# Six up products of the first shared unit moved beside the last attention batch

## The reference

```python
q = (layernorm(x) @ Wq.T) * scale ; k = ctx @ Wk.T ; v = ctx @ Wv.T      # 16 heads of 16
scores = sigmoid(einsum('blhd,bshd->bhls', q, k))                       # 8 x 16 x 512 x 1601
x = x + einsum('bhls,bshd->blhd', scores, v).reshape(B, L, E) @ Wo.T
n = layernorm(x)
# 16 experts: each takes its 64 best tokens of every batch (softmax of n @ gate_w.T)
h = gelu(x_tok @ Wg.T) * (x_tok @ Wu.T) ; out[tokens] += (h @ Wd.T) * weight
# one shared expert over all tokens
shared = (gelu(n @ Ws_g.T) * (n @ Ws_u.T)) @ Ws_d.T
return x + out + shared
```

## Time and profile before

| | |
|---|---|
| median of three runs | 1318.85 us (1317.76 to 1321.44) |
| profiled execution | 1318.16 us, span 1316.2 us |
| mean granted TensorE clock | 0.996 |
| PE busy | 1288.5 us (98%), 10172 matmuls |
| ACT busy | 984.2 us (75%) |
| DVE busy | 725.8 us (55%) |
| POOL busy | 285.6 us (22%) |
| chain that ended last | PE 85%, ACT 6%, DVE 3%, issue 3%, DMA 2% |

### The profile page before, as it was taken

One profiled execution on the slowest core, in us unless ns is written; L12 is line 12 of the kernel. 1 busy time (PEld: TensorE's weight loads), 2 busy tenths in 40 slices (PEclk: granted clock), 3 DMA queues, 4 the chain that ended last, 5 costly groups with the idle time before them and its releaser, 6 DMA issues.

```text
span 1316.2 us, 25441 instructions
## 1 busy us (share of the span) xinstructions
PE 1288.5 (98%) x10172; PEld 772.7 (59%) x10172; DVE 725.8 (55%) x1371; ACT 984.2 (75%) x1148; POOL 285.6 (22%) x288
## 2 busy tenths in 40 slices
PE   8899999999999999999999999999999999999997
PEld 6455444354444544444444453226888888888887
DVE  6375375376357437537535633204559777777773
ACT  4678999989998998998999889995232355555553
POOL 2000020021003002002000200220000567777635
PEclk9899999999999999999999999999999999999999
DMA  7784885775777587478567648624533577777854
GB/s 227 153 181 141 134 172 169 118 156 166 138 134 192 128 129 172 156 126 153 169 129 154 138 103 129 134 82 144 193 123 103 179 200 190 190 188 190 195 109 48
DMA packets 119637, 198.67 MB, mean 151 GB/s; under 512 B 22592, under 2 KB 71744, under 8 KB 119520
## 3 DMA queue, kind: packets, MB, share of 16 engines
q1 hardware_dynamic: 99680, 163.08, 52.5%
q0 software_dynamic: 19648, 33.72, 12.5%
q10 hardware_dynamic: 192, 0.26, 0.1%
HBM read 120.22 MB, written 63.47 MB: 140 GB/s over the span
## 4 chain that ended last, share of the span: by engine, by line
PE 85%; ACT 6%; DVE 3%; issue 3%; DMA 2%; SPq 1%; POOL 0%; POOLq 0%; DVEq 0%; ACTq 0%
PE score L1786 19%; PE score L1699 17%; PE acc L1728 13%; PE misc L1728 13%; PE score L1804 10%; ACT probs L860 6%; PE score L1530 5%; PE score L1544 5%; PE score L1553 1%; DMA keys<-key_scr 1%; PE score L1571 1%; SPq L548 1%; PE score L1634 0%; DMA norm_t_scr<-nt_lo 0%; POOL out L798 0%
## 5 line engine op out<-in xcount | busy, mean ns | idle before, releaser
L860 ACT ACTIVATE probs<-score 128x1024 f32<-128x1024 f32 (+1 forms) x832 | 788.4, 1034 | 84.6 <-PE score L1699 78.8
L1699 PE MATMUL score<-queries,keys 48*128 48x512 f32 (+1 forms) x1664 | 313.1, 439 | 13.4 <-DMA keys<-key_scr 5.6
L1699 PEld LDWEIGHTS score<-queries,keys 48*128 48x128 f32 (+1 forms) x1664 | 139.0, 180 | 288.0 <-ACT probs L860 220.6
L1728 PE MATMUL acc<-probs,values 128*32 128x512 f32 (+1 forms) x1664 | 212.4, 603 | 0.5 <-ACT probs L860 0.2
L1728 PE MATMUL misc<-probs,values 128*32 128x512 f32 (+1 forms) x1664 | 207.1, 600 | 2.0 <-ACT probs L860 0.9
L1004 DVE TENSOR_REDUCE whole<-score 128x512 f32<-128x1024 f32 (+1 forms) x75 | 77.0, 1026 | 205.3 <-PE score L1530 128.6
L713 POOL DMA_DIRECT2D ctx_raw<-ctx_t x32 | 23.4, 733 | 653.0 <-DVE ctx_lo L982 569.3
L870 ACT ACTIVATE gelu<-score 128x512 f32<-128x512 f32 (+1 forms) x100 | 57.2, 582 | 96.0 <-PE score L1786 95.4
L785 POOL DMA_INDIRECT gathered<-norm_scr,gather_row x64 | 81.3, 1270 | 197.2 <-DVE gather_row L1337 181.4
L1786 PE MATMUL score<-tok_hi,gu_hi 128*128 128x512 f32 (+1 forms) x400 | 120.7, 383 | 0.0
L1786 PE MATMUL score<-tok_lo,gu_hi 128*128 128x512 f32 (+1 forms) x400 | 120.0, 381 | 0.0
(11 more groups left out here) (248 smaller groups left out, 1563.6 us busy)
## 6 DMA issues: line engine op xcount, KB each, us to landing
keys<-key_scr SPq DMA_DIRECT2D x186, 200.2 KB, 7.9
key_scr<-key_parts SPq DMA_DIRECT2D x45, 512.0 KB, 8.1
gu_raw<-w_gu SPq DMA_DIRECT2D x17, 1024.0 KB, 6.8
ctx_raw<-ctx_t POOLq DMA_DIRECT2D x24, 512.0 KB, 5.1
queries<-query_scr SPq DMA_DIRECT2D x180, 64.0 KB, 2.8
d_raw<-w_d SPq DMA_DIRECT2D x17, 512.0 KB, 8.7
query_scr<-query_parts SPq DMA_DIRECT2D x15, 512.0 KB, 9.0
norm<-xn SPq DMA_DIRECT2D x224, 32.0 KB
```

The costliest lines, as they stand in the source:

```text
L860: act.activation(probs[0:rows, (n + 1) % RING, 2 * pair:2 * pair + 2, :], score[SLOT[k]][0:rows, :, :], ACT.Sigmoid, scale=SCALE).then_inc ...
L1699: mm = pe.matmul(score[SLOT[k]][0:rows, g, :], keys[quarter % KEY_RING][of, pair, P * st:P * st + rows], queries[half][of, e, pair, :], st ...
L1728: mm = pe.matmul(sums_bank[n // NST % 2][32 * c:32 * (c + 1), :], values[b % 2][0:rows, st, half, c, :], probs[0:rows, (n + 1) % RING, c, ...
```

## The change

Six of the products of unit 0 (gate and up tile of hidden tiles 0, 1 and 2) become products of the new kind U in the list of batch 7. They are made as 64-row halves into score slots, and VectorE adds the halves into the SBUF tile early_up, which lies where the third key buffer was. ScalarE's gelu and VectorE's hidden product of those three tiles read early_up in place of the PSUM banks. SP loads set 0 and unit 0's rows at pair 10 of batch 7, and unit 1's rows before the last quarter's scores end. CLOSING is a new string, with O 6 0 and O 6 1 three pairs later and the six U products behind pairs 51, 55, 69, 79, 95 and 99. The first O product of batch 7 comes after hidden tile 3's products, the second between unit 1's first two tiles.

```diff
+UPS_EARLY = 3
+UPS = [("U", B - 1, w, f) for f in range(UPS_EARLY) for w in range(2)]
+def full_of(n):
+    return FT * n - UPS_EARLY
@@ def beside(b):
                 ("T", c, 0), ("T", c, 1), ("Q", c, 0), ("K", c, 0, 2)]
+    else:
+        out += UPS[:2]
     if b:
         out += [("G", b - 1)]
...
+    else:
+        out += UPS[2:]
-CLOSING = ("SSSWWSSSWWSSTSSWSSSWWSSTSSWSSWSSWSSWSSWSWSSWSSWSSWSSWSSWSSWSWSSWSSWSSWSWSSWSSWSSWSWSSWS"
-           "SWSSWTSSWSSWSSWSSWSWSSWSSWSSWSSWSSWSSWSSWSSWSSWSSWSSWSSWSSWSSWSSWSSWSSWW")
+CLOSING = ("SSSWWSSSWWSSSWWSSTSSWSSSWWSSTSSWSSWSSWSSWSSWSWSSWSSWSSWSWSSWSSWSSWSWSSWSSWSSWSTSSWSSTSS"
+           "WSSSWWSSSWWSSSWTSSWSTSSWSSSWWSSSWWSSTSSWSSSWWSSSWWSSSWWSSSWWSSTSSWSSTSWSSSWWWW")
@@ SP, steps of the last batch
+                        if q == 5 and b + 1 == B:
+                            sp.wait_ge(misc_copied, COUNT["V", B - 1, NCH - 1, 0])
+                            keys_written(KEY_ORDER[-1])
+                            for half in range(2):
+                                sp.wait_ge(query_written[half], 16 * (B - 1 + half))
+                            sp.wait_ge(quad_done, QPB * (B - 1))
+                            load_weights(0, 0)
+                            sp.wait_ge(nt_stored, STORE * (B - 2))
+                            load_tokens(0)
@@ SP, behind the steps
-            load_weights(0, 0)
-            sp.wait_ge(nt_stored, STORE * (B - 1))
-            load_tokens(0)
-            sp.wait_ge(quad_done, QUADS)
-            load_tokens(1)
-            load_weights(1, 1)
+            sp.wait_ge(scores_done, GROUPS * (QUARTERS - 1))
+            load_tokens(1)
+            sp.wait_ge(quad_done, QUADS)
+            load_weights(1, 1)
+            sp.wait_ge(nt_stored, STORE * (B - 1))
@@ ScalarE, gelus(n, quarters)
+                    if n == 0 and f < UPS_EARLY:
+                        act.wait_ge(misc_copied, COUNT["U", B - 1, 0, f])
+                        of = early_up[:, 0, S * f:S * (f + 1)]
+                    else:
+                        act.wait_ge(g_full, full_of(n) + f + 1)
@@ ScalarE, units
                 gelus(n, (0, 1))
+                if n == 0:
+                    act.wait_ge(quad_done, QUADS)
                 hidden_hi(n, n % 2, (0, 1))
@@ VectorE
+            def early_ups(task):
+                _, _, w, f = task
+                dve.wait_ge(misc_full, COUNT[task])
+                if f == 0:
+                    dve.wait_ge(scores_done, GROUPS * (QUARTERS - 2))
+                dve.tensor_reduce(early_up[:, w, S * f:S * (f + 1)], score[SLOT[task]].rearrange("p e s -> p s e"),
+                                  AX_X, ALU.add).then_inc(misc_copied, 1)
@@ TensorE
+            def up_halves(task, bank):
+                _, _, w, f = task
+                pe.wait_ge(set_split, 1)
+                pe.wait_ge(tok_in[0], 32)
+                for j, (a, c) in enumerate(PRODUCTS):
+                    for k in range(KC):
+                        for e, rows in enumerate(ROW_TILES):
+                            mm = pe.matmul(bank[:, e, :], (gu_hi, gu_lo)[a][0][rows, w, k, P * f:P * (f + 1)],
+                                           (tok_hi, tok_lo)[c][0][rows, k, :],
+                                           start=(j == 0 and k == 0), stop=(j == 2 and k == KC - 1))
+                return mm
@@ up
-                        wait_past(pe, (gelu_done, hidden_done)[w], FT * n + f - 1)
+                        if FT * n + f >= UPS_EARLY + 2:
+                            pe.wait_ge((gelu_done, hidden_done)[w], FT * n + f - 1)
@@ TensorE, units
-            pe.wait_ge(set_split, 2)
-            pe.wait_ge(tok_in[0], 32)
-            up(0, 0, 0, (0, 1))
-            product(AFTER[0])
-            up(0, 0, 0, (2,))
-            product(AFTER[1])
-            up(0, 0, 0, (3,))
-
-            pe.wait_ge(tok_in[1], 32)
-            up(1, 1, 0, (0, 1))
+            up(0, 0, 0, range(UPS_EARLY, FT))
+            product(AFTER[0])
+            pe.wait_ge(tok_in[1], 32)
+            up(1, 1, 0, (0,))
+            product(AFTER[1])
+            up(1, 1, 0, (1,))
+            pe.wait_ge(set_split, 2)
             down(0, 0, 0)
```

More of the change, by code:

```diff
@@ L295, in build @@
             values.append(sa("values1", [P, NST, 2, 4, 2 * HD]))
-            keys = [sa(f"keys{i}", [P, 2, TP + 2], F32R) for i in range(KEY_RING)]
+            keys = [sa(f"keys{i}", [P, 2, TP + 2], F32R) for i in range(KEY_RING - 1)]
+            with ExitStack() as keys_stage:
+                keys.append(sbuf(keys_stage)(f"keys{KEY_RING - 1}", [P, 2, TP + 2], F32R))
+            early_up = sa("early_up", [P, 2, TP + 2])
             queries = [sa(f"queries{i}", [P, 2, 2, S], F32R) for i in range(2)]
@@ L318, in build @@
             d_raw = [d_raw0, sb("d_raw1", [P, FT, D])]
+            resid_in0 = sb("resid_in0", [P, TT, D])
             tok_hi = [tok_hi0, sb("tok_hi1", [P, KC, S], F32R)]
@@ L324, in build @@
             d_lo = [d_lo0, sb("d_lo1", [P, FT, D], F32R)]
-            gathered = [sb(f"gathered{i}", [P, TT, D]) for i in range(2)]
+            gathered0 = sb("gathered0", [P, TT, D])
             gelu = sb("gelu", [P, 2, S])
@@ L330, in build @@
             result = [sb(f"result{i}", [P, TT, D]) for i in range(2)]
-            resid_in = [sb(f"resid_in{i}", [P, TT, D]) for i in range(2)]
+            gathered = [gathered0, sb("gathered1", [P, TT, D])]
+            resid_in = [resid_in0, sb("resid_in1", [P, TT, D])]
             logits = sb("logits", [P, TT, B, E])
@@ L570, in second_queries, with load_weights, load_tokens @@
                                      ).then_inc(queries_in[0], 16)
+            def load_weights(s, slot):
+                sp.dma_start(gu_raw[slot][:].rearrange("p w k f -> p (w k) f"),
+                             w_gu[s].rearrange("w (k p) f -> p (w k) f", p=P)
+                             ).then_inc(set_in[slot], 16)
+                sp.dma_start(d_raw[slot][:], w_d[s].rearrange("(t p) d -> p t d", p=P)
+                             ).then_inc(set_in[slot], 16)
+            def load_tokens(b):
+                for part, tile in enumerate((tok_hi, tok_lo)):
+                    sp.dma_start(tile[b % 2][:].bitcast(F32), norm_t_scr[part][b]).then_inc(tok_in[b % 2], 16)
             first_keys(0)
@@ L621, in _ @@
                             stack_keys(4 * b + 5)
[L623 to L633, removed]
             def load_resid(b):
                 sp.dma_start(resid_in[b % 2][:], resid_scr[b]).then_inc(resid_read[b % 2], 16)
-            sp.wait_ge(misc_copied, COUNT["V", B - 1, NCH - 1, 0])
-            keys_written(KEY_ORDER[-1])
-            for half in range(2):
-                sp.wait_ge(query_written[half], 16 * (B - 1 + half))
-            sp.wait_ge(quad_done, QPB * (B - 1))
-            load_weights(0, 0)
+            sp.wait_ge(scores_done, GROUPS * (QUARTERS - 1))
+            load_tokens(1)
+            sp.wait_ge(quad_done, QUADS)
+            load_weights(1, 1)
             sp.wait_ge(nt_stored, STORE * (B - 1))
-            load_tokens(0)
-            sp.wait_ge(quad_done, QUADS)
-            load_tokens(1)
-            load_weights(1, 1)
             sp.wait_ge(post_stored, STORE * (B - 1))
@@ L679, in _ @@
                         sp.wait_ge(nt_stored, STORE * B)
-                    sp.wait_ge(u_full, FT * n)
+                    sp.wait_ge(u_full, full_of(n))
                     load_tokens(n + 1)
@@ L886, in hi_parts @@
                     if last_unit is not None:
-                        act.wait_ge(u_full, FT * (last_unit + 1))
+                        act.wait_ge(u_full, full_of(last_unit + 1))
                     act.activation(gu_hi[slot][:].rearrange("p w k f -> p (w k f)"),
@@ L1191, in copy_out @@
                     gate_logits(b)
+                elif kind == "U":
+                    early_ups(task)
                 else:
@@ L1278, in hidden_products @@
                     now = FT * n + f + 1
-                    dve.wait_ge(u_full, now)
+                    _, cols = piece(n, f)
+                    of = u_bank[:, f % 2, cols]
+                    if n == 0 and f < UPS_EARLY:
+                        dve.wait_ge(misc_copied, COUNT["U", B - 1, 1, f])
+                        of = early_up[:, 1, S * f:S * (f + 1)]
+                    else:
+                        dve.wait_ge(u_full, full_of(n) + f + 1)
                     dve.wait_ge(gelu_done, now)
                     wait_past(dve, hid_split, now - 2)
-                    _, cols = piece(n, f)
-                    dve.tensor_tensor(hidden[:, f % 2, cols], gelu[:, f % 2, cols], u_bank[:, f % 2, cols],
+                    dve.tensor_tensor(hidden[:, f % 2, cols], gelu[:, f % 2, cols], of,
                                       ALU.mult).then_inc(hidden_done, 1)
@@ L1660, in product @@
                     mm = query_halves(task[2], bank)
+                elif kind == "U":
+                    mm = up_halves(task, bank)
                 elif kind == "T":
```

9 lines of the change are left out of this document (4 added, 5 removed).

## The result

The changed kernel is slower: median 1321.93 us against 1318.78, 22 runs each, a ratio of 1.0027 with a 95% interval of 1.0018 to 1.0035. The profiled execution has a span of 1318.9 us against 1316.2. The forecast was 1315.8 with a range to 1320.0, so it is wrong in direction, and by 6 us.

The account below looks back on a forecast made before the run. ScalarE's sigmoids were taken to bound the kernel before 899 us, TensorE alone after. -6.05 + 2.3 + 0.7 = -3.05 us took the profiled 1318.16 to 1315.1, stated as 1315.8 for the median; range 1312.3 to 1320.0.

Parts of the forecast that it names:

- The first product's weights: Last batch, pair 51: GpSimd's weight split ends at 849.3, TensorE asks at 849.1; wait 0.7 us, bounds 0 and 3.
- Each such us is a stall of the same length on TensorE: Last batch: each us the norm store lands late stalls TensorE one us, with no room to recover.
- the backlog runs to about 829: DMA queue ahead of batch 6's norm store: 2.5 MB at 380 GB/s; the store may land 0 to 2 us late.
- Rival (c): First up product waits for the weight split; a loss if it ends after 852.9; six us late gives 1321.1; chance 0.07.
- The rule on the shared interfaces: GpSimd contends with VectorE's two-input instructions; two norm-split subtractions, 0.7 us each, would add to the stall, giving 1317.2.
- The six products and the new order: Last batch: six products of 1.38 us each and a new order string lengthen it by 2.3 us, bounds -0.3 and +8.3.
- the count of 97.7 us: TensorE's counted work in the last batch with the six products, above ScalarE's 94.6, so TensorE sets the pace.
- The unit stage: Behind T, the last sum's end: six up tiles fewer save 8.2 us, less waits of 1.75 and 0.4: 6.05 us.
- the new wait: Unit stage, ahead of unit 1's second up tile: TensorE waits 1.75 us for hidden tile 3, whose bank it overwrites.
- The table load: Start of the unit stage: ScalarE's table load of 1.28 us ends at T + 0.2 and stays hidden.
- the moved loads: Set 0's load, issued early, doesn't hold SP; unit 1's rows, loaded ahead of T, cost 0.
- the forecast's own sum: Whole kernel: -6.05 unit stage, +2.3 last batch, +0.7 weight wait, -3.05 us in all.

Follow-up runs that it names:

- experiment 3: Changed kernel with the loads of set 0 and unit 0's rows issued behind batch 6's norm store; ratio to the kernel before 1.0017.
- experiment 5: Changed kernel with VectorE's split of batch 6's turned norm moved from quad 22 to quad 34 of batch 7; ratio to the kernel before 1.0038.
- experiments 2: Changed kernel with 16 spare matmuls on TensorE ahead of the first early product's wait for its split weights; ratio to the kernel before 1.0037.
- experiment 6: Changed kernel with both the 16 spare matmuls in the weight wait and VectorE's norm split at quad 34; ratio to the kernel before 1.0001.
- experiment 11: Version of experiment 7 with each early product made of two matmuls instead of twelve; one run, last-batch stretch 96.99 us against 96.21.
- experiment 12: Kernel before with only the last batch's new order of scores and sums, without the six products; ratio to the kernel before 1.0018.
- experiment 4: Kernel before with only the loads of set 0 and unit 0's rows moved ahead as in the change; ratio to the kernel before 0.9996.
- experiment 7: Changed kernel with GpSimd's weight split ahead of the placing transfers and VectorE's norm split at quad 34; ratio to the kernel before 0.9982.
- experiment 1: Changed kernel with GpSimd's gate/up weight split of set 0 ahead of batch 6's norm placing transfers; ratio to the kernel before 0.9983.

## Why the prediction was wrong

The 9.1 us by which the last batch grew come apart along the experiments, taken away in this order: 102.50 to 102.33 VectorE's hold, 0.2; to 100.09 the half clock, 2.2; to 96.21 the wait for the weights, 3.9; to 93.38 the products and their order, 2.8.

- **The step that failed** is "The first product's weights": "I take 0.7 us; bounds 0 and 3", and with it "Each such us is a stall of the same length on TensorE". The wait was 3.8 us. Of the 3.1 that were missing, 2.5 come from the store: I let it land 0 to 2 us late behind the 2.5 MB and counted 0.5, and it was 3.6 late (experiment 3 gives 3.5 of them back), though issued 0.6 earlier than I had it. TensorE asking at 848.7 instead of 849.1 makes another 0.4. Behind the store's lateness stands a rate: the sum let the 2.5 MB run at 380 GB/s from their issue, "the backlog runs to about 829". The DMA engines, full already, moved 122 to 141 GB/s until 824, and the last load landed at 832.1.
- **The price of the wait** was the other half of the step. One us for one holds for the wait itself (3.9 us of stretch for the 3.9 that the spare matmuls had filled), but behind it the clock fell and cost 2.2 more. I had looked for a stall's length and not for what TensorE does behind it. Rival (c) had the place, the cause and the direction right, with a chance of 0.07; it wanted a split later than 852.9 for a loss, and with the clock behind the wait 852.35 was enough.
- **The rule on the shared interfaces** was weighed on the wrong side. I let GpSimd's split pay for VectorE's subtractions. The trace shows the reverse: gu_lo took 4.58 us against 4.57, and nt_lo, begun 0.24 us behind it, 4.88 against 0.69, ending 0.54 us behind gu_lo; the next, begun behind d_lo, ended 0.54 us behind that as well. Of GpSimd's work only the cast d_hi, issued while nt_lo ran, took longer, 1.50 us against 1.04. The Trainium skill (SBUF — State Buffer, the section on its two separate sides) says the pair of ports is locked by whichever begins first and the other stands still for the whole instruction. By that rule the later one pays, and the trace agrees. In the change this cost 0.2 us by experiment 5, but in experiments 2 and 3 it made stalls of 2.53 and 3.10 us, and with the wait filled it is worth 4.0 us (experiment 6 against 2).
- **The six products and the new order**: +2.3 forecast, +2.8 measured with every wait away. A product took 1.39 us against 1.38. The size is right. That it is TensorE's time, as the count of 97.7 us had it, experiments 11 and 12 do not show; the estimate behind experiment 12 speaks for the order and the slots.
- **The unit stage**: 6.05 us forecast, 6.3 measured (416.5 - 410.2). With T = 908.62, the down product stands at T + 13.0 against 12.9, the second turned norm at T + 22.1 against 22.2 (930.70 - 908.62), and the new wait is 1.4 us between the matmuls (1.9 for the weight load) against 1.75.
- **The table load** stayed hidden, and the moved loads by themselves cost nothing (experiment 4), as forecast.

Put into the forecast's own sum: -3.05, + 3.1 for the longer wait, + 2.2 for the clock, + 0.2 for VectorE's hold, + 0.5 for products and order, - 0.25 for the unit stage, is + 2.7 us; the profiled executions differ by 2.7. With the wait and the half clock away, the change is close to its forecast: experiment 7 is at -0.18%, 2.4 us (interval 0.8 to 3.8), against 3.05 forecast with 0.7 of waiting in it. That the size of the products came out so near is in part luck, if the count behind it does not hold.

## What to carry to other kernels

When work is moved ahead, follow its operands' way back over every queue with the old slack of each written beside it: here the load had slack, but the store ahead of the placing ahead of the split had none left. Take the rate of a transfer from the rows of the stretch in which it will run, not from a later one. Price a stall of the matmul engine with the clock behind it, not by its length alone, and look for a second wait behind the first before taking the first away. A moved piece of GpSimd work should be held against what VectorE does in the same microseconds.

## What was not expected of the hardware

- TensorE's granted clock falls without a long stop. In experiments 11 and 12 it went to 0.55 (858 to 860 us) and 0.61 (856 to 860 us) behind gaps of at most 0.65 and 0.42 us each, with TensorE busy for 6.2 and 6.9 of the 8 us ahead of those stretches, and in the kernel before, which fills the same stretch more evenly, it stayed at 1.00.
- A VectorE copy with one SBUF operand is held by GpSimd's subtraction too: in experiment 1 nt_hi, begun 0.09 us behind d_lo, took 2.57 us (0.42 alone) and ended 0.3 us behind it.
- Sixty matmuls fewer made a stage 0.8 us longer, in one execution (experiment 11).
- DMA engines that were full (share 0.96 to 1.05) moved 122 to 141 GB/s from 816 to 824 us and 377 to 401 GB/s from 824 to 832.
